# A relational graph layer on one core: TensorE's main loop over steps written out as straight-line code

## The reference

```python
h = jnp.maximum(_layernorm(x, axis=-1), 0.0)
hx = jnp.einsum('ni,rio->rno', h, weight)           # 8 relations
msg = hx[edge_type, src]
agg = jax.ops.segment_sum(msg, dst, num_segments=num_nodes)
return x + agg * 0.5 ** 0.5 + h_bias + (h @ loop_weight) * 0.5 ** 0.5
```

## Time and profile before

| what | value |
|---|---|
| runs without profile, median | 2342.75 us |
| profiled execution, its span (the page gives no other time of it) | 2975.6 us |
| TensorE matmul, busy | 1792.1 us (60%) in 10566 matmuls |
| GpSimd, busy | 1699.8 us (57%) |
| VectorE, busy | 1201.0 us (40%) |
| ScalarE, busy | 520.9 us (18%) |
| granted TensorE clock, mean | 0.767 of full |
| DMA, mean over the span | 97 GB/s |

### The profile page before, as it was taken

The page is one execution under the profiler, slowest core; times in us unless marked ns, Lnnn a source line. Parts: engine busy times, 40 slices in busy tenths (PEclk is TensorE's granted clock), DMA queues, the critical chain, the costliest instruction groups (busy, mean ns, idle before and its releaser), DMA issues.

```text
span 2975.6 us, 39409 instructions
## 1 busy us (share of the span) xinstructions
PE 1792.1 (60%) x10566; PEld 1293.5 (43%) x10566; DVE 1201.0 (40%) x2675; ACT 520.9 (18%) x590; POOL 1699.8 (57%) x1687
## 2 busy tenths in 40 slices
PE   0046665665666666666675665666666665755667
PEld 0024444454444444444454444444444444443445
DVE  9834333343344343333343333333443334333433
ACT  4401111111111111111111111111111111111111
POOL 5466556565565565556555556466566555565553
PEclk9997777777777777777777767777777777777778
DMA  6533323333333333333333323233333333333232
GB/s 221 180 119 97 86 79 104 90 94 92 90 93 94 95 94 92 87 91 96 88 94 89 92 80 100 76 97 97 89 99 96 86 92 93 89 97 88 81 89 64
DMA packets 128701, 287.90 MB, mean 97 GB/s; under 512 B 31806, under 2 KB 71738, under 8 KB 125614
## 3 DMA queue, kind: packets, MB, share of 16 engines
q0 software_dynamic: 79728, 217.82, 26.0%
q1 hardware_dynamic: 47122, 57.12, 5.9%
q10 hardware_dynamic: 1836, 12.80, 1.0%
HBM read 262.01 MB, written 25.60 MB: 97 GB/s over the span
## 4 chain that ended last, share of the span: by engine, by line
PE 46%; issue 26%; DVE 12%; another core or an unknown queue 10%; DVEq 4%; DMA 1%; POOL 1%; ACT 0%; POOLq 0%; ACTq 0%; SPq 0%
PE ps_out L789 31%; PE sums L815 14%; DVE ring L683 4%; DVE onehot L641 2%; DVEq L672 2%; DVE result L662 1%; DVE stats L546 1%; DVE ring L652 1%; POOL rows L370 1%; PE ps_out L794 1%; DVEq L683 1%; DVE mv L563 1%; DMA rows<-h_table,index_now 1%; DMA xg<-x 0%
## 5 line engine op out<-in xcount | busy, mean ns | idle before, releaser
L370 POOL DMA_INDIRECT rows<-h_table,index_now x1661 | 1631.7, 982 | 1179.3 <-PE sums L815 531.0
L683 DVE TENSOR_TENSOR ring<-ring,sums 128x256 f32 x1661 | 700.3, 422 | 1715.5 <-remote 915.8
L789 PE MATMUL ps_out<-w_sb,stage 128*128 128x256 f32 x3072 | 1176.8, 503 | 208.7 <-issue 199.8
L815 PE MATMUL sums<-onehot,rows 128*128 128x128 f16 x6644 | 747.5, 245 | 869.5 <-issue 569.1
L815 PEld LDWEIGHTS sums<-onehot,rows 128*128 128x128 f16 x6644 | 526.0, 110 | 1189.6 <-issue 828.1
L789 PEld LDWEIGHTS ps_out<-w_sb,stage 128*128 128x128 f32 x3072 | 698.1, 250 | 378.0 <-issue 309.3
L452 ACT COPY index_now<-src_i 128x8 int32 (+1 forms) x196 | 38.8, 198 | 2128.0 <-PE sums L815 1687.0
L641 DVE TENSOR_TENSOR onehot<-lane,slot 128x768 f16<-128x768 f16 (+1 forms) x293 | 270.7, 924 | 0.4 <-issue 0.4
L459 ACT COPY stage<-ring 128x2048 f32 (+1 forms) x96 | 182.2, 1898 | 227.2 <-DVE carry L654 147.8
L462 ACT COPY ring<-zeros 128x2304 f32 (+1 forms) x96 | 202.8, 2112 | 10.9
L794 PE MATMUL ps_out<-w_sb,own_hT 128*128 128x256 f32 x384 | 112.6, 419 | 0.0
(11 more groups left out here) (52 smaller groups left out, 244.0 us busy)
## 6 DMA issues: line engine op xcount, KB each, us to landing
rows<-h_table,index_now POOLq DMA_INDIRECT x1661
own<-h_table SPq DMA_DIRECT2D x97, 128.0 KB
own_x<-x SPq DMA_DIRECT2D x97, 128.0 KB
out<-result SPq DMA_DIRECT2D x97, 128.0 KB
xg<-x SPq DMA_DIRECT2D x12, 1024.0 KB, 6.1
h_table<-tg ACTq DMA_DIRECT2D x12, 1024.0 KB, 8.2
w_sb<-weight SPq DMA_DIRECT2D x2, 1024.0 KB
dst_i<-dst SPq DMA_DIRECT2D x1, 833.0 KB, 10.5
```

The costliest lines, as they stand in the source:

```text
L370: nc.gpsimd.indirect_dma_start(out=rows[:, k, :], out_offset=None, in_=table[:, :], in_offset=bass.IndirectOffsetOnAxis(ap=index_now[:, k: ...
L683: nc.vector.tensor_tensor(window, window, sum_of(k).rearrange("p (a w) -> p a w", w=W), ALU.add).then_inc(added, 1)
L789: nc.tensor.matmul(ps_out[:, 0:D], stage[:, m, :], w_sb[:, h, r, :], start=(m == 0), stop=False)
L815: last = nc.tensor.matmul(sum_of(k)[:, h * P:(h + 1) * P], rows[:, k, part * D + h * P:part * D + (h + 1) * P], onehot[:, k, :], start=(pa ...
```

## The change

The loop on the device becomes a loop of the Python program that writes the kernel. Steps 3 to 96 of TensorE's program stand one after the other, with `s` a number in each. `tensor_step` has an `isinstance(s, int) and s == 0` kind of test in one place (L805, L785, L757); for s of 3 and more both kinds of `s` take the same branches. The matmuls, their order, the semaphores and what is waited for stay the same. The loops of the other engines stay.

```diff
@@ -862,7 +862,7 @@
                     if s == 2:
                         pe.wait_ge(s_w, 16 * (2 * H + 1))
                     tensor_step(s, K, s >= 2)
-                with pe.Fori(3, STEPS - 1) as s:
+                for s in range(3, STEPS - 1):
                     tensor_step(s, K, True)
                 tensor_step(STEPS - 1, K_LAST, True, 5)
                 own_rows(TILES - 2)
```

## The result

The kernel with the change takes 2347.40 us (median of 15 runs, 2342.43 to 2351.20), the kernel before beside it 2341.09 us (median of 15, 2338.98 to 2342.92). The ratio is 1.0025, with a 95% interval of 1.0017 to 1.0032. The change costs 6.3 us, and the interval leaves out 1.

A forecast was written before the change was run, and what follows sets the result against it. The prediction took GpSimd's issue of gathers to bound the kernel for about 98% of its time. Its terms, removed loop work, code fetch and contention, summed as 2342.75 + 0 + 0 + 0 = 2342.8 us, range 2322 to 2364 us.

The forecast's parts named there:

- a case that had 0.15: Whole kernel measurably slower, beyond about 0.2% (4.7 us): late code or the slower half of the VectorE-GpSimd beat shift; chance 0.15.
- its own sign: Whole kernel: the prediction is wrong if the time leaves 2338 to 2347.5 us.
- Its other sign: GpSimd's mean gather, 982 ns before, tells whether the VectorE-GpSimd beat shifted; 0.012 us more or less is 20 us.
- What bounds the kernel: GpSimd's issue of gathers, one per 1.25 us, a floor of 2250 us; binds about 98% of the timed run.
- The stalls: Waits of VectorE, TensorE and GpSimd in the profile, some 670 us of GpSimd's span, taken to belong to the profiled execution.
- The 38 us of waits for TensorE at half clock: GpSimd waiting some 2.6 us in each of about 15 low-clock steps of 98; 38 us together.
- The 55 us of held time: GpSimd gathers longer than the 949 ns median, overlapping VectorE's one-hots; 55 us added to the floor, making 2305 us.
- Removed branch and register work: TensorE's loop branch and register instructions, gone 94 times; taken to save 0, at most 38 us.
- Fetched code does not stop TensorE: TensorE's 83 to 115 code blocks are fetched ahead, costing 0; upper bound 110 us.
- rival C: Code arrives late and stops TensorE at block edges, once a step: +55 us, 2398 us; chance 0.10.
- Contention: Gather rows sharing a DMA engine with a code block land up to 0.96 us late; cost 0, bound 110 us.
- rival B: VectorE-GpSimd beat shifts, changing one-hot and gather overlaps: 19 us, to 2324 or 2362 us; chance 0.07 faster, 0.05 slower.

The follow-up runs named there:

- e1: TensorE's steps 3 to 96 as two trips over 47 written-out steps, waits against registers, against the kernel before: 2959.6 against 2962.0 us, ratio 1.000.
- e4: Kernel before with one extra 16 KB DRAM-to-DRAM DMA a step on SyncE, against the kernel before: ratio 1.0018 (0.9997 to 1.0039).
- e10: Two trips over 47 written-out steps, registers kept, in a second batch, against the kernel before: 2979.4 against 2986.9 us, ratio 0.9988.
- e11: Kernel before with one extra 16 KB DMA a step, in a second batch, against the kernel before: ratio 0.9895 (0.9849 to 0.9940).
- e13: Kernel before with one extra 16 KB DMA a step, in a third batch, against the kernel before: ratio 0.9857 (0.9792 to 0.9921).
- e7: Kernel before, TensorE's loop kept, with VectorE's one-hots cut into 17 instructions a step in place of 3: 2267.7 us, ratio 0.9685 to before.
- e12: Two trips over 47 written-out steps, registers kept and code streamed, in a third batch, against the kernel before: 2345.25 against 2341.06 us, ratio 1.0023.
- e8: The change (TensorE's steps written out) with one-hots cut into 17 instructions a step, against the kernel before: 2268.7 us, ratio 0.9695.
- e6: The change itself measured again, against the kernel before: 2345.8 against 2341.3 us, ratio 1.0026 (1.0016 to 1.0035).
- e3: The change with one-hots cut into 17 instructions a step, in an earlier batch, against the kernel before: 2968.3 us, ratio 1.0019.
- run 94: Not a follow-up run: the words say that TensorE's loop body of one step is executed 94 times in the kernel before, 2341.09 us.

## Why the prediction was right, and where it was not

**The forecast, 2342.8 us and no change that can be told,** missed by 4.6 us, and by 6.3 us against the kernel before beside it. The measured 2347.4 us lies in the range, and the ratio lies just on the slower side of 0.2%, a case that had 0.15. It is also 0.1 us inside the 2338 to 2347.5 us beyond which the prediction was to be wrong by its own sign. Its other sign, the gathers' mean against 982 ns, could not be used: the mean is 1005 ns, by that rule 38 us slower, but the 982 ns come from a profile of the 2960 kind.

**What bounds the kernel** came out right, and more fully than stated: the floor was put at 2250 us from intervals of 1.25 us, and four profiles give 2255 to 2256 us.

**The stalls** were ascribed to the profiled execution. That is wrong in its cause: they come with the batch, and all runs of such a batch are as long as the profiled one (e1 to e4, e10, e11 and e13). The conclusion drawn from them, that the timed runs of 2342 us don't have them, was right, because it rested on the sum and not on their cause. What makes a batch of the 2960 kind is open.

**The 38 us of waits for TensorE at half clock** did not exist. GpSimd never waits beyond 0.31 us between gathers in any profile of the 2341 kind. The sum behind them took a step in which all of k = 8 to 16 runs at half clock. No such step occurs in the profile after: from the start of chunk 8's sums to that of chunk 16's TensorE takes 10.4 to 12.5 us in every step of the loop's range, where eight intervals at half clock would be 17.7, and the index copy is done at least 5.7 us before gather k = 8 starts. The 55 us of held time in the earlier trace rows had been read from a trace in which GpSimd stands still for a fifth of the time. There 127 gathers start during a one-hot, in the profile after 244. Without those waits the held time is 87 to 92 us in the change and, by the sum, 83 us in before. The term of the sum was mis-sized: 38 us of supposed waits were 28 us of held time, 6 us of floor (a gather and its gap are 0.949 + 0.305 = 1.254 us, not 1.25), 2 us outside the span and 2 us by which before was faster in 15 runs than in 3. A lever of some 74 us was hidden by it, which e7 then took.

**Removed branch and register work: 0.** No gain came of it, as forecast. The beat is 1.14 us in both, and e12, with the registers back, costs about the same as the change. The Trainium skill ("Advanced Engine Details and Errata", Control Flow Timing) gives about 108 ns for a compare-and-branch, and an estimate from it would make the change 10 us faster. The measurement decides: with all 94 branches gone the kernel is not faster but 6.3 us slower. That their absence shifts something else is not excluded.

**Fetched code does not stop TensorE: 0.** Right, rival C is out. The fetch runs ahead of the program, 91 blocks pass, the intervals between chunks stay, and TensorE's idle time is the same with and without the stream (573.1 and 574.7 us, e7 and e8). The Trainium skill ("Runtime: NRT & Kernel Launch", Instruction fetch mechanics) says that the next block is fetched while the present one runs, and the trace agrees.

**Contention: 0.** This is the term that most likely failed. It was priced by the slack of 6 us that GpSimd has against TensorE, and no such wait arose. But a landing that comes late can also move TensorE's chunk, VectorE's addition behind it and the one-hot behind that, and with it the one-hot's overlap with the next gather. The prediction had both halves, the contention here and the overlap in rival B, and dismissed B with the words that the phase "is set by landings, which TensorE's program doesn't move". Its code does move them, 0.7 to 0.8 us for 7% of the gathers. The size was 4 to 6 us, not B's 19. That the time stayed near the forecast is partly luck: nothing in the prediction kept the phase from costing more.

How far is this shown? Shown: what is above the floor is gathers held by one-hots (e7, and the count of holds); the cost is there with registers kept and code streamed (e12); the code's packets go with late landings. Not shown: that it is the fetched code and not the missing back edges; that the late landings lengthen the holds, for which the direct comparison above finds no sign; and that the cost goes when the one-hots are short (4.5 to 1.0 us, within the scatter of the runs). TensorE's granted clock is a further path that no run separates: its mean in the runs is 0.824 and 0.822 with streamed code (e6, e12) and 0.825 and 0.827 in before beside them. The extra load of e4 could not decide any of this, and the held time of before rests on a sum and not on a profile.

The Trainium skill ("GPSIMD Engine Reference", Key points) states that GpSimd shares its SBUF interfaces with VectorE, with contention by VectorE instructions that have two SBUF inputs. The trace agrees: the one-hot has two such inputs and holds the gather, and the addition with one input in PSUM held none of 620. The prediction used the rows alone and did not ask what the rule is worth when the one-hot is cut up.

## What to carry to other kernels

Where GpSimd issues gathers back to back, write down its floor (count x interval) first. What is above it is either waits or held time, and the two are told apart by whether the gathers' idle time or their busy time grows. It pays to cut long VectorE instructions with two SBUF inputs into pieces: here 3 a step became 17, VectorE worked some 95 us more, and the kernel became 3.1% faster than before. Writing out the loop of an engine that isn't the bound gave nothing here and cost 0.2 to 0.3%.

## What was not expected of the hardware

- One program takes two levels of time in different batches, 2341 and 2962 to 3004 us. At the higher one TensorE and VectorE stall for up to 12 us at a time (11.6 in e3) with no cause in the trace, while GpSimd's gathers keep their median of 946 to 949 ns. It is not the chip alone: one and the same chip took 2962 us for before in the batch of e1 and 2341 us in that of e12.
- A loop body of one step (108 matmuls) is run 94 times with at most one block of code fetched, and the program with a body of 47 steps in two trips fetches 95 blocks in all. Where between them the streaming begins was not tried.
- A gather that starts during a two-input VectorE instruction is longer by nearly what that instruction still has to run: 0.67 us for 0.79 left, 0.69 for 0.82 in the earlier trace rows, and 0.13 us less than what is left in the median of 212.
